# Node numbers, base weights and half-products moved to PSUM, and one of the fill's one-hots moved to GpSimd

## What is computed

```
edge_index = jnp.stack([src, dst])
x = _layernorm(x + L0(x, Wq, Wk, Wv, Wo, edge_index))             # transformer, 4 heads, x + attention inside
x = _layernorm(x + L1(x, weight, w_comp, ..., src, dst, type))    # relational, 16 bases, 86 edge types
x = _layernorm(x + L2(x, edge_weight, src, dst, 3))               # three times X = A X, A of edge weights
x = _layernorm(x + L3(x, edge_index, ...))                        # three GATv2 layers, 8 heads
```

## Time and profile before

| | us |
|---|---|
| median of 3 runs | 11181.7 (11179.84 to 11182.36) |
| profiled execution, its own time | 11180.74 |
| its span, first to last instruction | 11178.8 |
| TensorE busy (share, mean clock) | 7937.1 (71%, 0.837) |
| VectorE busy | 7409.1 (66%) |
| GpSimd busy | 4658.4 (42%) |
| ScalarE busy | 1583.1 (14%) |

### The profile page before, as it was taken

The page is one execution under the profiler, slowest core; times in us unless marked ns, Lnnn a source line. Parts: engine busy times, 40 slices in busy tenths (PEclk is TensorE's granted clock), DMA queues, the critical chain, the costliest instruction groups (busy, mean ns, idle before and its releaser), DMA issues. The chain is left out here.

```text
span 11178.8 us, 168009 instructions
## 1 busy us (share of the span) xinstructions
PE 7937.1 (71%) x33251; PEld 5848.5 (52%) x33252; DVE 7409.1 (66%) x14155; ACT 1583.1 (14%) x4852; POOL 4658.4 (42%) x4765
## 2 busy tenths in 40 slices
PE   0888869788888777775666655976664796666488
PEld 0788869667666444441344434654442565444256
DVE  2233346667764777770388877978887796888688
ACT  0222211222221000000111101111110111111011
POOL 1677710688882000000177750037774004777200
PEclk9999999899998555556699977979996897999698
DMA  6222241111113222227455563125555303555520
GB/s 24 52 58 58 58 49 38 31 35 36 36 35 19 83 83 83 83 83 305 162 137 137 137 114 70 30 74 137 137 137 101 62 28 98 137 137 137 97 44 23
DMA packets 1413037, 947.03 MB, mean 85 GB/s; under 512 B 916254, under 2 KB 1276695, under 8 KB 1412434
## 3 DMA queue, kind: packets, MB, share of 16 engines
q0 software_dynamic: 184960, 458.42, 18.9%
q1 hardware_dynamic: 1131794, 427.96, 16.2%
q10 hardware_dynamic: 96192, 59.54, 1.7%
HBM read 697.23 MB, written 248.11 MB: 85 GB/s over the span
## 5 line engine op out<-in xcount | busy, mean ns | idle before, releaser
L846 PE MATMUL ps<-rows,ohT 128*128 x7040 | 2181.5, 450 | 1380.8 <-DMA gx<-table_g,gi 660.8
L631 POOL DMA_INDIRECT gx<-table_g,gi x2640 | 2501.8, 948 | 801.9 <-issue 728.0
L846 PEld LDWEIGHTS ps<-rows,ohT 128*128 128x128 f32 x7040 | 1449.0, 248 | 1951.5 <-DMA gx<-table_g,gi 972.7
L1135 PE MATMUL ps<-work,oh 128*128 128x273 f32 (+1 forms) x7040 | 1778.4, 408 | 347.9 <-DVE oh L650 338.8
L1135 PEld LDWEIGHTS ps<-work,oh 128*128 128x128 f32 x7040 | 1340.5, 227 | 784.8 <-issue 436.5
L616 POOL COPY gi<-src_i 128x16 int32 (+1 forms) x280 | 64.8, 231 | 3953.0 <-POOLq L510 3900.6
L1611 PE MATMUL ps<-oh 128*128 128x196 f32 x2352 | 1072.9, 603 | 343.3 <-DVE oh L1595 342.7
L631 POOL DMA_INDIRECT gx<-table_r,gi x880 | 1158.7, 1317 | 261.8 <-issue 228.4
L735 DVE TENSOR_TENSOR work<-gx,ps 128x768 f32<-128x768 f32 x660 | 629.8, 954 | 731.7 <-PE ps L848 730.9
L1341 PE MATMUL ps<-work,oh 128*128 128x272 f32 x3520 | 961.1, 431 | 193.5 <-DVE work L1261 193.0
L1100 DVE TENSOR_TENSOR work<-rows,xl 128x1024 f32<-128x1024 f32 (+1 forms) x880 | 871.5, 990 | 323.0 <-DMA xl<-xs_g 147.1
(11 more groups left out here) (304 smaller groups left out, 8575.3 us busy)
## 6 DMA issues: line engine op xcount, KB each, us to landing
big<-dense_d SPq DMA_DIRECT2D x96, 784.0 KB
dense_d<-big SPq DMA_DIRECT2D x588, 98.0 KB
dense_d<-big ACTq DMA_DIRECT2D x588, 98.0 KB
gx<-table_g,gi POOLq DMA_INDIRECT x2640
xs_g<-gx SPq DMA_DIRECT2D x660, 64.0 KB
xl<-xs_g SPq DMA_DIRECT2D x660, 64.0 KB, 1.8
rows<-dense_d SPq DMA_DIRECT2D x48, 784.0 KB
type_d<-work SPq DMA_DIRECT2D x220, 96.0 KB
```

The lines of the kernel that those rows point to most:

```text
L631: pool.indirect_dma_start(m.gx[:, u, k, 0:w], None, table, bass.IndirectOffsetOnAxis(m.gi[:, odd, u * K + k:u * K + k + 1].bitcast(U32), 0 ...
L846: ins = nc.tensor.matmul(to, turned, rows, start=True, stop=not adds)
L1135: ins = nc.tensor.matmul(sums(u), m.oh[:, u, k, :], rhs(u % 2)[:, k, :], start=(k == 0), stop=(k == K - 1))
```

## The change

In the transformer walk `node_no` now is a part of PSUM (the bank behind the projections), filled once with `iota_row` before the walk; both the one-hot and the one-hot of types read it. In the relation walk the node numbers, the scaled base weights (`scales`, in place of `ac`) and the products that are reduced to the score (`hats`, in place of `lx`) lie in a PSUM bank that was free; `ac` and `lx` are gone from SBUF. In the dense fill GpSimd makes `his`, into the same ring of four slots. For that it copies four numbers of `v_hi` per turn of the loop to a fixed place, waits for its own copy, and in each visit waits until the product of four visits before is made. TensorE waits for both one-hots. The attention layers keep their code.

```diff
@@ allocate
-    m.ac = sb("ac", [P, 2, K, NBASE])
-    m.lx = sb("lx", [P, 2, K, D])
@@ logits
-    att_row, node_no = (m.psC[:, 0, 0:W3], m.psC[:, 0, W3:W3 + P]) if gat else (None, None)
+    att_row = m.psC[:, 0, 0:W3] if gat else None
+    node_no = m.psC[:, 0, W3:W3 + P] if gat else m.psA[:, 0, 512:512 + P]
...
-                        m.typ[:, u % 2, :, :], m.iota_b[:, 0:NREL].unsqueeze(1).to_broadcast([P, K, NREL]),
+                        m.typ[:, u % 2, :, :], node_no[:, 0:NREL].unsqueeze(1).to_broadcast([P, K, NREL]),
...
-                nc.vector.tensor_copy(node_no, m.iota_row[:, :]).then_inc(s("rows_set"), 1)
-                dve.wait_ge(s("rows_set"), 1)
+            nc.vector.tensor_copy(node_no, m.iota_row[:, :]).then_inc(s("rows_set"), 1)
+            dve.wait_ge(s("rows_set"), 1)
@@ relation_walk
+    scales = m.psT[:, 1, 0:2 * K * NBASE].rearrange("p (n k b) -> p n k b", n=2, k=K)
+    node_no = m.psT[:, 1, P:2 * P]
+    hats = m.psT[:, 1, 2 * P:4 * P].rearrange("p (n k d) -> p n k d", n=2, k=K)
...
-                one_hot(nc, m, g, slot).then_inc(s("node_hot"), 1)
+                one_hot(nc, m, g, slot, False, node_no).then_inc(s("node_hot"), 1)
...
-                y = m.lx[:, half, :, :]
+                y = hats[:, half, :, :]
...
-                nc.vector.tensor_reduce(m.a1[:, half, 0, :], m.lx[:, half, :, :], AX.X, ALU.add
+                nc.vector.tensor_reduce(m.a1[:, half, 0, :], hats[:, half, :, :], AX.X, ALU.add
...
-                nc.vector.tensor_tensor(m.ac[:, half, :, :], m.type_in[:, slot, :, D:TYPE_W],
+                nc.vector.tensor_tensor(scales[:, half, :, :], m.type_in[:, slot, :, D:TYPE_W],
...
-                                        m.ac[:, half, :, :].unsqueeze(3).to_broadcast(shape),
+                                        scales[:, half, :, :].unsqueeze(3).to_broadcast(shape),
...
+            nc.vector.tensor_copy(node_no, m.iota_row[:, :]).then_inc(s("numbers"), 1)
+            dve.wait_ge(s("numbers"), 1)
@@ dense_fill
-                                        m.v_w[:, bass.ds(v, 1)], ALU.is_equal, ALU.mult)
-                nc.vector.tensor_scalar(his[:, u, :], m.hi_no[:, :], m.v_hi[:, bass.ds(v, 1)], None, ALU.is_equal
-                                        ).then_inc(s("hot"), 1)
+                                        m.v_w[:, bass.ds(v, 1)], ALU.is_equal, ALU.mult).then_inc(s("hot"), 1)
...
+        @block.gpsimd
+        def _(pool):
+            numbers = m.lin[:, 0, 0:RING]
+
+            def body(i, u):
+                v = i * RING + u
+                if not u:
+                    need(pool, s("high"), v)
+                    nc.gpsimd.tensor_copy(numbers, m.v_hi[:, bass.ds(v, RING)]).then_inc(s("numbers"), 1)
+                    pool.wait_ge(s("numbers"), i + 1)
+                need(pool, s("made"), v - RING + 1)
+                pool.sem_inc(s("place"), 1)
+                nc.gpsimd.tensor_scalar(his[:, u, :], m.hi_no[:, :], numbers[:, u:u + 1], None, ALU.is_equal
+                                        ).then_inc(s("high"), 1)
+            groups(pool, body, turns)
...
                 pe.wait_ge(s("hot"), v + 1)
+                pe.wait_ge(s("high"), v + 1)
```

## The result

The kernel after takes 10737.3 us by the median (10731.7 to 10744.3, four runs) against 11180.8 us (11172.3 to 11182.4, four runs): a ratio of 0.9605, 95% interval 0.9588 to 0.9622, 443.5 us less. The forecast was 10778, 403 less. The profiled execution took 10736.09 us, its span is 10734.2.

What follows compares the result with a forecast made beforehand. No engine bounds the whole: GpSimd's gather queue sets both walks, a VectorE-TensorE loop the fill. 290 + 40 + 74 = 404 us less than the median gives 10778 us; 8 in 10 for 10640 to 10960.

Steps and rivals of the forecast that it cites:

- A loop of the two: Dense fill: VectorE waits 290 us for TensorE's product, so the two form a loop, spanning two visits.
- Transformer walk, 40 us: Transformer walk: unheld gathers bring 1161.5 us down to the attention walk's 1121.5, 40 us less, bounds 30 and 45.
- Relation walk, 290 us: Relation walk: fewer held gathers bring 1442.9 us to 1144, less 9 given back for jitter: 290 us, bounds 240 and 305.
- rule of squares: Both walks: gather loss per group goes with summed squared lengths of two-SBUF-input VectorE operations, factor 0.24; 9 us left.
- The errata sentence: Relation walk: 120 fixed cycles from PSUM against 58 from SBUF would add 65 ns to each of five VectorE instructions.
- Fill, 74 us: Dense fill: `his` on GpSimd makes a visit 1.14 us, 74 us less; bounds 135 less to 108 more.
- The hold of `spots`: Dense fill: GpSimd's `his` makes VectorE's `spots` wait, taken as 0.10 us in each span of two visits.
- The clock did not return: Rival, dense fill: denser products bring TensorE's clock back, fill 1000 us instead of 1415, total 10437; chance 0.10.
- TensorE limit the relation walk: Rival, relation walk: TensorE at a low clock sets it, gaining only 176 us, total 10892; chance 0.08.
- GpSimd as the bound: Rival, dense fill: slow `his` makes GpSimd the bound and the kernel slower, 11460 at 1.3 us; chance 0.06.
- The gather is not freed: Rival, both walks: one tensor left in SBUF still holds gathers, only the fill moves, total 11108; chance 0.06.
- The signs: Profile after, walks and fill: gathers about 1.2 us at most but the first, relation walk 1145 to 1155, `spots` held under `his`.

Runs made afterwards that it cites:

- e9: Kernel after, with VectorE adding the product of two visits back instead of one in the fill: 10543.6 us, ratio to before 0.9393.
- e12: Kernel after with the lag of two visits, `his` on VectorE in even visits and on GpSimd in odd ones: 10438.8 us, ratio to before 0.932.
- e1: Kernel before with the transformer walk's change alone: 11170.0 us, against 11196.0 of before on the same chip.
- e6: Kernel after, with the relation walk's first three one-hots, queued behind the memset, reading node numbers from SBUF again: 10751.1 us.
- e4: Kernel before with only the relation walk's scaled base weights moved to PSUM: 10915.3 us.
- e5: e4 with the score and the one-hot put ahead of the addition of `collect` in the relation walk: 10940.8 us.
- e8: Kernel after, with GpSimd computing each `his` twice in the fill, the first into an unused buffer: 11396.8 us.
- e2: Kernel before with the relation walk's change alone: 10903.0 us, against 11196.0 of before on the same chip.
- e11: Kernel after with the lag of two visits in the fill and `spots` reading node numbers from PSUM: 10538.6 us, ratio to before 0.9388.
- e10: Kernel after with the lag of two visits in the fill, but `his` on VectorE as before the change: 10484.1 us, ratio to before 0.9336.
- e7: Kernel after, with `spots` in the fill reading its node numbers from PSUM: 10719.6 us.

## Why the prediction was right, and where not

- **What bounds the kernel.** Right: GpSimd's queue set the walks, and freeing it moved them by 41 and 316 us. "A loop of the two" in the fill was right as well, and e9 to e12 show how much it was worth; the prediction read the loop and did not ask about its span.
- **Transformer walk, 40 us.** Measured 41.1; e1 gave 37.5 of walk by itself. The attention walk as the floor of the term was the right row.
- **Relation walk, 290 us.** Measured 316, above the bound of 305. Three pieces of the sum, 31.7 us together, were off. The 13.7 us of the first gather were put on the memset and left in; e6 shows that the one-hots behind the memset caused them, and those are changed. (Back in e6 they cost 6.3 us of walk, since VectorE and TensorE took most of the rest anyway.) The 9 us left for the small products by the rule of squares are not there (in e4 the issues but for the first are 1.7 us too long together, in after none is over 1.07). The 9 us given back for jitter were not needed: TensorE, at 275 of 280 us and 1.00, kept up. Against them stand 5.5 us (1127.0 against the attention walk's 1121.5), where GpSimd now waits for the outer product: 31.7 - 5.5 = 26. (The lower bound, 240, does not follow from its own 5.35 us a group, which make a walk of 1191 us and a gain of 252; nothing hung on it.)
- **The rule of squares.** Wrong, though it fitted both walks of before, with 0.235 (rounded up to 0.24 in the prediction) and 0.25. Two fits were no proof; why the two came out so alike, no run shows. e4 and e5 have the same instructions and differ by 42 us.
- **The errata sentence.** The outer product from PSUM takes 2.292 us against 2.29, the one-hot 0.68 as before, `y` 0.299 against 0.29: 3 to 10 ns, not the 65 ns that the page's figures gave (the Trainium skill, "VectorE: DVE Perf Modes", The TRN2 errata). The measurement decides.
- **Fill, 74 us.** Measured 117, inside the bounds (-135 to +108). The term that I mis-sized most, `his` on GpSimd, 0.42 us against a measured 0.78, did the least harm. The hold of `spots` that I hung on it, 0.10 us in two visits, came out at 2 x (0.383 - 0.342) = 0.08, with 0.342 the mean before. The prediction's step from a long `his` to a long hold was wrong: `his` of 0.65 was to cost 0.41 us, 0.78 cost 0.08. That is 0.02 of the 0.07 us by which two visits came out shorter than forecast. The way through TensorE, from the last operand to the addition, is not the rest. I had read it for the first visit of a turn, 1.39 us, and used it for both halves; for the third visit it was 1.29 already before (4201.67 - 4200.38), and after it is 1.39 and 1.29 again (4001.27 - 3999.88, 4003.38 - 4002.09), all four by the medians over the fill too:

```profile
4200.06 0.32 DVE L1595 TENSOR_SCALAR oh<-gx,big 128x196 f32<-128x196 f32 x1
...
4201.67 0.42 DVE L1586 SCALAR_TENSOR_TENSOR big<-big,gx,ps 128x196 f32<-128x196 f32 x1 [0.48 <-PE ps L1611]
```

```profile
3998.97 0.42 DVE L1590 SCALAR_TENSOR_TENSOR big<-big,gx,ps 128x196 f32<-128x196 f32 x1 [0.79 <-PE ps L1630]
3999.52 0.36 DVE L1597 TENSOR_SCALAR oh<-iota_row,big 128x128 f32<-128x128 f32 x1
```

What got shorter is VectorE's step from one turn of the loop to the next: from the addition to the next `spots` once in four visits, 0.65 us before (4202.32 - 4201.67) and 0.55 after (3999.52 - 3998.97), which is 0.05 in two visits. My sum held this step at its old length, and at 0.10 in two visits where it was 0.16. VectorE has one instruction fewer a visit there; whether that is the reason, no run shows.
- **The rivals.** The clock did not return in the fill of after (0.50), nor did TensorE limit the relation walk (1.00). GpSimd as the bound is real, but only in e8. "The gather is not freed" fell with e1 and e2. The clock did come back, in part or whole, in other kernels (0.65 to 0.67 in e9 and e11, 0.87 in e10, 1.00 in e12), and e12's 0.84 us a visit is near that rival's 0.85. But the rival had the clock bring that rate, and there the lag did: e10's turn is as long at 0.50 as at 1.00. In e7's spells a turn is shorter with the clock, 3.54 against 4.38 us.
- **The signs.** As forecast: issues under 1.2 us, the transformer walk 1120.4, the wait for rows VectorE's largest in the relation walk, the wait for the product largest in the fill. Not as forecast: the first gather, a relation walk of 1127 for 1145 to 1155, and `spots` held wherever `his` runs. A `his` above 0.7 us was named as a sign of being wrong; it came, and the fill was faster than forecast all the same.

The total was right to 41 us partly because errors offset: 26 us too little in the relation walk and 43 in the fill, less 29 us that no term held, of which 20 are the clock in the projection.

## What to carry to other kernels

When a VectorE instruction with two SBUF inputs overlaps GpSimd's indirect DMAs, put one input in PSUM if a bank is free; here that cost at most 10 ns and gave 357 us, and look also at what stands queued behind a long instruction, not only at the long one. Before an operation is moved to another engine, see whether any engine is full: if none is, the loop between them is the limit, and one more visit of lag (211 us here, 390 on the fill of the kernel before) is worth more than the move (117), which can even turn into a loss once the lag is there (61). A loss by overlap is a matter of phase, so a rule fitted to totals does not carry over; ask at which moment the held instruction asks.

## What the runs showed of the hardware that I had not expected

- Inside the walks a gather on GpSimd is held only if about 0.12 us after its start VectorE is inside an instruction with two SBUF inputs, and, with the outer product, only if that began at least 0.045 us before the gather (211 of 211; of those that began later, none of 91). It then ends 0.82 us after the instruction does (2714.36, 900.55, 2603.83, and the first gather of e6, 1967.54: all to 0.01 or 0.02 us).
- An 11.39 us memset of VectorE does not hold it; a one-hot queued behind the memset does, for 13.7 us.
- GpSimd's tensor_scalar with a pointer takes 0.77 us for 128x196 elements, where its affine select took 0.29 for 128 and VectorE needs 0.32 for the same work. A `spots` from SBUF that lies wholly inside it can keep its 0.34 us.
- The granted clock in the fill was 0.50 at 1.10 us a visit, 0.65 and 0.67 at 0.92 and 0.91, 0.87 at 0.87 and 1.00 at 0.84, with the same product per visit in all. Which of the differences between these kernels the clock follows was not tested. What 1.00 instead of 0.50 gives depends on what bounds the loop: 0.84 us in a turn of four visits that meets a spell in e7, nothing in the turns of e10 and e11 that lie at one level throughout.
